# A pre-norm attention and FFN block on one core: 273 softmax denominators summed by VectorE, tokens in two buffers by turns, bias added in place

## The reference, cut to what matters

```
x = x + attn(layernorm(x));  x = x + ffn(layernorm(x))
attn: q, k, v = split(x @ Wqkv)
      num = exp((rotated q) (rotated k)^T / 4)
      den = sum over all keys of exp(q k^T / 4)       # plain q and k, no mask
      y = where(causal, num / den, 0) @ v;  return y @ Wout + bout
ffn:  relu(x @ Ws1)^2 @ Ws2 + routed part (trunc of the top-2 weights)
```

## Time and profile before

| | |
|---|---|
| median of 3 runs | 1646.12 us (1645.99 to 1646.13) |
| the profiled execution | 1646.03 us, its span 1644.4 us |
| ACT busy | 97% |
| PE busy (modelled ends, pipelined) | 91% |
| DVE busy | 51% |
| POOL busy | 32% |
| mean granted TensorE clock | 0.997 |

### The profile page before, as it was taken

How to read it: one execution, slowest core, us unless ns; L and a number is a source line. 1 busy time by engine, 2 the same in 40 slices (tenths; PEclk the granted TensorE clock), 3 DMA queues, 4 the chain that set the end, 5 groups by cost and what they waited for, 6 DMA issues and landing times.

```text
span 1644.4 us, 26290 instructions
## 1 busy us (share of the span) xinstructions
PE 1503.6 (91%) x8594; PEld 614.6 (37%) x8594; DVE 845.8 (51%) x1949; ACT 1591.2 (97%) x2651; POOL 530.2 (32%) x919
## 2 busy tenths in 40 slices
PE   8899999999999989999899999989989999999988
PEld 6334333333333333333333332433333333333325
DVE  5334434665346653566445554565534665346515
ACT  2999999999999999999999999999999999999995
POOL 3334133432234322343333323324223432234310
PEclk9999999999999999999999999999999999999999
DMA  5532233331434313343233333333243331433310
GB/s 164 154 104 87 78 106 116 121 107 50 132 116 132 116 36 126 116 132 106 78 110 119 113 96 105 114 116 97 84 141 110 121 99 62 132 106 116 103 39 27
DMA packets 95392, 172.10 MB, mean 105 GB/s; under 512 B 15696, under 2 KB 82256, under 8 KB 83152
## 3 DMA queue, kind: packets, MB, share of 16 engines
q1 hardware_dynamic: 94656, 169.55, 33.0%
q10 hardware_dynamic: 592, 0.79, 0.2%
HBM read 111.55 MB, written 58.72 MB: 104 GB/s over the span
## 4 chain that ended last, share of the span: by engine, by line
ACT 88%; PE 6%; issue 3%; DVE 1%; POOL 0%; DVEq 0%; DMA 0%; POOLq 0%
ACT scores L546 57%; ACT probs L556 27%; ACT probs L558 3%; PE scores L621 2%; PE y_ps L650 1%; PE side L602 1%; PE side L660 1%; PE scores L628 0%; POOL v_sb L424 0%; DVEq L931 0%; DMA qk_parts<-parts 0%; PE scores L679 0%; PE scores L808 0%; PE scores L669 0%; PE side L679 0%
## 5 line engine op out<-in xcount | busy, mean ns | idle before, releaser
L546 ACT ACTIVATE scores<-scores 128x1024 f32<-128x1024 f32 x1024 | 1068.0, 1124 | 16.1 <-PE scores L621 15.7
L621 PE MATMUL scores<-stack 96*128 96x512 bf16 x2048 | 579.9, 382 | 63.0 <-ACT scores L546 36.3
L556 ACT ACTIVATE probs<-scores 128x1024 f32<-128x1024 f32 x512 | 491.8, 1113 | 1.7 <-PE scores L628 1.7
L628 PE MATMUL scores<-stack 96*128 96x512 bf16 (+3 forms) x1536 | 332.4, 328 | 43.3 <-ACT scores L546 35.0
L443 POOL TENSOR_SCALAR_AFFINE_SELECT probs<-probs 128x256 f32<-128x256 f32 (+1 forms) x640 | 241.2, 404 | 378.5 <-ACT probs L556 218.0
L650 PE MATMUL y_ps<-probs,v_sb 128*32 128x512 f32 (+3 forms) x3072 | 329.0, 500 | 5.1 <-POOL probs L443 5.1
L621 PEld LDWEIGHTS scores<-stack 96*128 96x128 bf16 x2048 | 153.5, 97 | 460.6 <-ACT scores L546 201.3
L546 ACT ACTIVATION_READ_ACCUMULATOR scores<-scores 128x1 f32 x1024 | 302.7, 296 | 0.0
L453 POOL TENSOR_TENSOR parts<-rest,parts 128x512 bf16<-128x512 f32 x124 | 143.2, 1155 | 293.3 <-DVE parts L998 293.3
L628 PEld LDWEIGHTS scores<-stack 96*128 96x128 bf16 x1536 | 117.1, 98 | 290.2 <-ACT scores L546 150.0
L451 POOL TENSOR_TENSOR rot<-raw,cos_sb 128x512 f32<-128x512 f32 x62 | 89.4, 1441 | 388.5 <-DVEq L1008 388.5
(11 more groups left out here) (140 smaller groups left out, 1150.8 us busy)
## 6 DMA issues: line engine op xcount, KB each, us to landing
stack<-qk_parts SPq DMA_DIRECT2D x756, 128.0 KB, 2.6
qk_parts<-parts SPq DMA_DIRECT2D x127, 384.0 KB, 2.6
out<-x_mid SPq DMA_DIRECT2D x32, 256.0 KB, 2.9
x_in<-in_L_attn_x SPq DMA_DIRECT2D x7, 1024.0 KB, 5.3
stack<-qk_parts SPq DMA_DIRECT2D x18, 64.0 KB, 2.3
x_in<-in_L_attn_x SPq DMA_DIRECT2D x2, 512.0 KB, 4.5
probs<-in_L_attn_Wqkv SPq DMA_DIRECT2D x1, 512.0 KB, 5.8
cos_sb<-in_cos SPq DMA_DIRECT2D x1, 512.0 KB, 6.5
```

What stands on the lines that cost most here:

```text
L546: nc.scalar.activation(src, src, ACT.Exp, scale=SCALE, accum_out=den[:, g % 2, i, j:j + 1]).then_inc(exp_done, 1)
L556: nc.scalar.activation(probs[:, chunk % 2, j, :], src, ACT.Exp, scale=SCALE).then_inc(exp_done, 1)
L621: mm = nc.tensor.matmul(tile[:, half * HALF:(half + 1) * HALF], q[:, j, i * P:(i + 1) * P], k[:, j, half * HALF:(half + 1) * HALF], start= ...
L628: mm = nc.tensor.matmul(tile[:, col:col + n], k[:, h, i * P:(i + 1) * P], q[:, h, q0:q0 + n], start=True, stop=True)
```

## The change

1. 273 of the 1024 den steps no longer accumulate. ScalarE writes their exponentials to one of two new SBUF tiles (`sum_tiles`) with a plain activation, and VectorE adds the two halves with one scalar_tensor_tensor that has an accumulator output (`sum_den`), three steps later in its queue (`SUM_LAG`). ScalarE waits, before it writes one such tile, until the one two before was summed. Per unit: 7, 8, 9 and 11 of them in the four groups, 8 in the first and 3 in the last unit.
2. All tables of the order are new.
3. The product with the cosines moves from POOL to VectorE (read from PSUM), the shuffle moves from the `turn` to the `qk` job, and `raw` is gone.
4. Tokens are in two buffers used by turns; attention is added in place; the bias is added in place by POOL in unit 0 of the batch (8 separate instructions at steps 2 to 37). The load of the next tokens no longer waits for POOL's copy; from the second batch on it waits for `tokens_used`.
5. A drain before each reciprocal; `ones` has one column; several tiles share memory.

The core of the diff:

```diff
-ORDER = [5, (0,), 4, (1,), 3, (2,), 7, (3,), 6, (4,), 7]
-ORDER_FIRST = [16, (0,), 1, (1,), 1, (2,), 1, (3,), 1, (4,), 12]
-ORDER_LAST = [0, (0,), 4, (1,), 0, (2,), 7, (3,), 11, (4,), 10]
+ORDER = [5, (0,), 5, (1,), 3, (2,), 7, (3,), 5, (4,), 7]
+ORDER_FIRST = [14, (0,), 0, (1,), 3, (2,), 0, (3,), 9, (4,), 6]
+ORDER_LAST = [1, (0,), 1, (1,), 3, (2,), 2, (3,), 18, (4,), 7]
+SUM_SLOTS, SUM_LAG = 2, 3
+SUMMED = [
+    (6, 7, 10, 12, 16, 17, 27),
+    (1, 4, 15, 21, 22, 24, 25, 27),
+    (5, 9, 11, 16, 18, 19, 21, 26, 28),
+    (3, 6, 9, 11, 12, 15, 21, 22, 25, 27, 28),
+    (2, 5, 17),
+    (1, 7, 12, 17, 19, 23, 24, 26),
+]
...
 SIDE = [
-    {0: ("v", 0), 4: ("qk", 0), 8: ("v", 1), 12: ("v", 2), 14: ("turn", 1), 20: ("qk", 2), 28: ("turn", 3),
-     30: ("v", 3), 35: ("norm", 0), 38: ("norm", 1)},
...
+    {0: ("qk", 0), 4: ("v", 0), 8: ("v", 1), 12: ("v", 2), 18: ("turn", 1), 21: ("qk", 2), 24: ("turn", 3),
+     30: ("v", 3), 38: ("norm", 0), 41: ("norm", 1), 47: ("acc", 0)},
...
+    {1: ("qk", 0), 6: ("ffn", 1), 10: ("route", 2), 11: ("turn", 1), 13: ("qk", 2), 18: ("ffn", 2),
+     24: ("norm", 0), 26: ("turn", 3), 28: ("norm", 1), 31: ("acc", 0), 33: ("acc", 1), 38: ("ffn", 3),
+     40: ("acc", 2), 47: ("xt", 0), 49: ("xt", 1)},
...
-COPY = (1, 43)
+BIAS = (0, (2, 7, 12, 17, 22, 27, 32, 37))
...
+        sum_tiles = sb("sum_tiles", [P, SUM_SLOTS, C])
+        tokens = [sb(f"tokens{i}", [P, NB, D]) for i in range(2)]
...
+                        if not first:
+                            sp.wait_ge(tokens_used, at(b, 1, 0))
+                            sp.sem_inc(held["sp"], 1)
+                        sp.dma_start(tokens[(b + 1) % 2][:, :, :], x_v[b + 1]).then_inc(x_loaded, 16)
...
-                if t % 2 == 0:
-                    pool.wait_ge(raw_ready, at(b, 8, 2 * g + t // 2 + 1))
-                    nc.gpsimd.tensor_tensor(rot[:, :], raw[:, :], cos_sb[:, t // 2 * HALF:(t // 2 + 1) * HALF], ALU.mult)
...
+                        if g == BIAS[0] and s in BIAS[1]:
+                            if s == BIAS[1][0]:
+                                pool.wait_ge(xn_ready, at(b, 4, 4))
+                            block = tokens[b % 2][:, BIAS[1].index(s), :]
+                            nc.gpsimd.tensor_tensor(block, block, bias[:, :], ALU.add).then_inc(biased, 1)
...
+                    if s in SUM_AT[unit_of(b, g)]:
+                        k = sums_ahead(b, g) + SUM_AT[unit_of(b, g)][s]
+                        if k >= SUM_SLOTS:
+                            act.wait_ge(summed, k - SUM_SLOTS + 1)
+                        nc.scalar.activation(sum_tiles[:, k % SUM_SLOTS, :], src, ACT.Exp, scale=SCALE).then_inc(exp_done, 1)
+                        return
...
-                    nc.vector.tensor_copy(raw[:, :], side).then_inc(taken["qk"], 1)
-                    dve.drain().then_inc(raw_ready, 1)
-                    split(0, raw[:, :])
+                    nc.vector.tensor_copy(rest[:, :], side)
+                    nc.vector.tensor_tensor(rot[:, :], side, cos_sb[:, cols], ALU.mult).then_inc(taken["qk"], 1)
+                    settle()
+                    nc.vector.tensor_copy(parts[:, 0, 0, :], rest[:, :])
+                    nc.vector.stream_shuffle(turned[:, :], rest[:, :], PARTNER)
+                    settle()
+                    nc.vector.tensor_tensor(rest[:, :], rest[:, :], parts[:, 0, 0, :], ALU.subtract)
                     middle(0)
                 else:
-                    nc.vector.stream_shuffle(turned[:, :], raw[:, :], PARTNER)
-                    settle()
...
+            def sum_den(b, g, s):
...
+                dve.wait_ge(exp_done, at(b, G * NSTEP, g * NSTEP + s + 1))
+                nc.vector.scalar_tensor_tensor(tile[:, 0:HALF], tile[:, 0:HALF], 0.0, tile[:, HALF:C], ALU.add, ALU.add,
+                                               accum_out=den[:, g % 2, i, j:j + 1]).then_inc(summed, 1)
...
             def reciprocals(b, g):
                 dve.wait_ge(exp_done, at(b, G * NSTEP, (g + 1) * NSTEP))
+                settle()
...
+                        if s - SUM_LAG in SUM_AT[unit_of(b, g)]:
+                            sum_den(b, g, s - SUM_LAG)
```

More of the change, by code:

```diff
@@ L90, in unit_of, with summed_steps, sums_ahead @@
     return G if b == B - 1 and g == G - 1 else G + 1 if b == 0 and g == 0 else g
+SUM_SLOTS, SUM_LAG = 2, 3
+SUMMED = [
[6 rows of a table added]
+]
+def summed_steps(steps, chosen):
+    dens = [s for s, x in enumerate(steps) if x[0] == "den"]
+    return {dens[d]: k for k, d in enumerate(chosen)}
+SUM_AT = [summed_steps(steps, chosen) for steps, chosen in zip(STEPS, SUMMED)]
+def sums_ahead(b, g):
+    return sum(len(SUM_AT[unit_of(n // G, n % G)]) for n in range(b * G + g))
 PIECES = [(0, 0), (0, 1), (1, 0), (1, 1), (2, 0), (2, 1), (2, 2), (3, 1), (3, 0), (3, 2), (4, 0), (4, 1)]
 PV_STEPS = [
[6 rows of a table removed]
[6 rows of a table added]
 ]
@@ L104 @@
 Y_FIRST, Y_LAST = [(0, 0), (3, 0)], [(3, 1), (4, 1)]
-TAKE_Y = [47, 42, 37, 42, 36, 39]
+TAKE_Y = [39, 35, 39, 44, 33, 40]
 LOW_LAG = 3
-RECIPROCALS = (32, 25, 16, 25)
+RECIPROCALS = (30, 35, 9, 24)
 SIDE = [
-    {0: ("v", 0), 4: ("qk", 0), 8: ("v", 1), 12: ("v", 2), 14: ("turn", 1), 20: ("qk", 2), 28: ("turn", 3),
-     30: ("v", 3), 35: ("norm", 0), 38: ("norm", 1)},
[L119 to L128, removed]
-    {0: ("qk", 0), 4: ("v", 0), 8: ("turn", 1), 10: ("v", 1), 14: ("qk", 2), 18: ("v", 2), 22: ("turn", 3), 24: ("v", 3)},
@@ L130 @@
+    {1: ("acc", 3), 4: ("xt", 2), 5: ("xt", 3), 8: ("qk", 0), 15: ("ffn", 4), 18: ("ffn", 5), 21: ("turn", 1),
+     23: ("qk", 2), 28: ("turn", 3), 34: ("ffn", 6), 37: ("ffn", 7)},
+    {1: ("acc", 3), 5: ("ffn", 4), 7: ("ffn", 5), 10: ("ffn", 6), 19: ("ffn", 7), 36: ("end", 0),
+     39: ("end", 1), 40: ("end", 2), 47: ("end", 3), 48: ("end", 4)},
+    {2: ("qk", 0), 8: ("v", 0), 11: ("turn", 1), 12: ("v", 1), 18: ("qk", 2), 22: ("v", 2), 26: ("turn", 3),
+     29: ("v", 3)},
 ]
@@ L257, in block @@
         chunk_used = sem("chunk_used")
+        summed = sem("summed")
         y_ready = sem("y_ready")
@@ L482, in batch @@
                     for s in range(NSTEP):
-                        if (g, s) == COPY:
-                            if not first:
-                                pool.wait_ge(x_acc_used, at(b, 1, 0))
-                            else:
-                                pool.wait_ge(x_first, 16)
-                                pool.wait_ge(x_loaded, 16)
-                            for i in range(NB):
-                                last_copy = nc.gpsimd.tensor_tensor(x_acc[:, i, :], x_in[:, i, :], bias[:, :], ALU.add)
-                            last_copy.then_inc(x_copied, 1)
+                        if g == BIAS[0] and s in BIAS[1]:
[3 more added lines that the diff above has]
+                            nc.gpsimd.tensor_tensor(block, block, bias[:, :], ALU.add).then_inc(biased, 1)
                         for c in DIAGONALS:
@@ L816, in end_tile @@
                     pe.wait_ge(weight_ready, at(b, 1, 1))
[L817 removed]
+                    mm = nc.tensor.matmul(side[0:1, 0:NB], ones[:, :], weight[:, :], start=True, stop=True)
                 mm.then_inc(end_full, 1)
@@ L1074, in acc_tile @@
                 src = side.rearrange("p (i d) -> p i d", i=2)
-                into = x_mid if pair else x_acc
-                nc.vector.tensor_tensor(into[:, blocks, :], src, x_acc[:, blocks, :], ALU.add).then_inc(taken["acc"], 1)
+                into = x_mid if pair else tokens[b % 2]
+                nc.vector.tensor_tensor(into[:, blocks, :], src, tokens[b % 2][:, blocks, :], ALU.add).then_inc(taken["acc"], 1)
                 if pair:
                     if t == 3:
-                        dve.drain().then_inc(x_acc_used, 1)
+                        dve.drain().then_inc(tokens_used, 1)
                     else:
@@ L1150, in end_tile @@
                     blocks = slice(2 * t, 2 * t + 2)
-                    nc.vector.tensor_tensor(x_mid[:, blocks, :], side.rearrange("p (i d) -> p i d", i=2), x_acc[:, blocks, :],
+                    nc.vector.tensor_tensor(x_mid[:, blocks, :], side.rearrange("p (i d) -> p i d", i=2), tokens[b % 2][:, blocks, :],
                                             ALU.add).then_inc(end_taken, 1)
```

60 lines of the change are left out of this document (30 added, 30 removed), and 12 rows, old and new, of the table PV_STEPS.

## The result

The change takes 1631.42 us (median of 5 runs, 1628.03 to 1635.59) against 1646.12 us before: ratio 0.991, 95% interval 0.990 to 0.993. It is faster by 14.7 us where 33 were forecast, and the time lies outside the stated range of 1608 to 1624 us. The profiled execution is one of 1631.42 us, span 1629.8.

A forecast was written before the change was run, and what follows sets the result against it. ScalarE's own pace was taken to bound the kernel (ACT busy for 97% of the span). From 1646.0 us, minus 34.7 for the accumulator read-outs, plus 1.5 for late sums, came 1612.8 us; range 1608 to 1624 us.

The forecast's parts named there:

- 273 denominators without accumulator: On ScalarE's path: each plain activation saves the 0.127 us accumulator read-out, 34.7 us in all.
- The sums on VectorE: Each sum costs VectorE 0.86 us (0.70 to 1.73), 235 us for all 273.
- The cosine product moves: From POOL to VectorE: 43 us more on VectorE, 89 less on POOL; with shorter neighbours, VectorE nets 16 us less.
- VectorE in all: VectorE's total load: 1065 us (1020 to 1302) of some 1613, 66%, leaving room on average.
- Where a late sum would be felt: ScalarE waiting for a free sum tile at 23 close-spaced places: 1.5 us charged, bounds 0 and 12 us.
- Tokens and bias: Token loads and in-place bias on SP's and POOL's queues: no effect on the time.
- TensorE, no lack: In unit 0, the heaviest, TensorE needs 43 us of the 48.3 that ScalarE needs, so it holds nothing up.
- The first unit: First numerator after 14 denominators, waiting some 2 us for DMA; the 1.0 us its 8 sums count was left in.
- A: VectorE's answer comes late, behind POOL's masks or long jobs; ScalarE or TensorE waits: 1618 to 1630 us, chance 0.15.
- the likeliest case: The forecast itself, ScalarE's saving nearly whole: 1608 to 1618 us, chance 0.75.

The follow-up runs named there:

- run 1: The change, with each of the 273 sums on VectorE adding one column instead of 512 (denominators then wrong): 1620.99 us.
- run 2: The change, with one product with v (chunk 3, piece 1) of unit 0 at step 40 in place of 38: 1623.89 us.
- run 3: The change, with POOL's 8 bias additions early, at steps 2 to 19 of unit 0: 1622.79 us.
- run 7: The change, with each sum done by a VectorE reduction over 1024 columns instead of adding two halves: 1634.04 us.
- run 5: The change without any sum, all 1024 denominators accumulated by ScalarE: 1657.25 us, ratio 1.0051 to the kernel before.
- run 13: The change without any sum and with the first acc job back at step 3 of unit 1: 1647.62 us, ratio 1.0013 to before.
- run 17: The change, with unit 0's product with v at step 40, the bias early and a few small filler matmuls on TensorE: 1617.35 us, ratio 0.9813 to before.
- run 11: The kernel before, with only the first acc job moved from step 3 of unit 1 to step 47 of unit 0: 1646.55 us, ratio 1.0001.
- run 14: The change, with three small unused matmuls at each of ten steps where TensorE had least to do: 1630.15 us.
- run 9: The change, with unit 0's product with v at step 40, the bias early and acc at step 4 of unit 1: 1620.73 us.

## Why the prediction was wrong

- *273 denominators without accumulator, 34.7 us*: right. Measured 273 x 0.126 = 34.4, and the idle time before these activations is 0.1 us.
- *The sums on VectorE, 0.86 us* (its three terms add up to 0.85): right, 0.77 + 0.08. Alone a sum takes 0.68, by the rows of batch 3, and a plain addition 0.70. The Trainium skill, in Vector Engine (DVE) Microarchitecture Reference, section Points that are easy to get wrong, gives half throughput for two SBUF sources that are not bf16. These rows do not show it: halved, a sum would take some 1.2 us (an estimate from that page).
- *The cosine product moves*: right on VectorE (0.68; the subtraction 0.69). POOL lost 55 us of busy time, not 89, as its other instructions became longer: the third parts by 26 us, the bias by 9.
- *VectorE in all*: 1018 us, below the 1065 and 2 us under the lower bound of 1020. The lengths of its rows grew by some 218 us, near the 219 that I had; its busy time, which counts overlapping rows once, grew by 172. I had added lengths to a busy time.
- *Where a late sum would be felt, 1.5 us*: **this step failed.** I looked for the price only where ScalarE waits for `summed`, and there it is indeed nothing. I had measured the exclusion and used it only to make the sum dearer. It works the other way too: a sum holds POOL, and POOL carries the masks, behind which TensorE and then ScalarE stand. 10.2 us, shown by runs 1, 2, 3 and 7.
- *Tokens and bias, nothing*: failed with it. I said what it removes from SP's queue and not what it puts in POOL's: two bias additions in front of the masks of chunk 3. I also did not put the new step 38 of the product beside step 35 of its last numerator, though both stood in the diff.
- *TensorE, no lack*: right for its amount of work, and blind to its clock. The kernel before had 0.997, and I took it for given; the new order has stretches after which it falls. By run 5 against 13 the change without sums lost some 9 us to it. In the change itself it is 4 to 5, an estimate from 1.1 us per 0.001 and a mean clock over its runs of 0.992 against 0.996 to 0.997.
- *The first unit*: the first numerator started at 51.18 where I had 51.2. But the unit's shortage grew by 2.1 us, 3.1 of its 6.4 in front of the first numerator (I had some 2); its sums gave 1.0 and it took 1.1 us longer.
- The rivals: A had the right witnesses (POOL's masks behind the sums) and the wrong place, ScalarE's wait for a slot; its 1618 to 1630 is near the result. I gave it 0.15 and cut the range in its middle. What the forecast wanted exists: with both misplacements mended and the clock kept up (run 17) the time is 1617.4 us, inside the likeliest case.

Open: what, besides the stretch that the moved acc job thins, decides in which batches the clock falls there (run 11 has the same thin stretch and one dip), and the 5 us of waits of 0.1 to 0.4 us spread over the units.

## What to carry to other kernels

When work moves to an engine that can shut another out, price it on both: list what is queued on the other engine behind each instruction that can be held up, and who waits for that. When an order is rewritten, look at what is *thinned* as well as at what is crowded: TensorE's clock fell after light stretches, though not after all of them, and a few useless matmuls in them kept it up. Whether those pay is less clear: beside tight steps they cost what they saved (run 14), and away from them the gain over a kernel without them was within the scatter (runs 9 and 17). And if ScalarE accumulates, take the price of it from distances between starts (0.126 us), not from the row of the read-out (0.2 to 0.37 us).

## What the runs showed of the hardware

- A VectorE instruction with two SBUF inputs and a POOL instruction that reads SBUF shut each other out, in both directions: a sum of 0.68 us took 1.64 behind POOL, a third part of 1.16 us took 1.61 behind a sum. With one SBUF input (the reduction, 1.21 us for 1024 columns) or with one column, POOL's rows were undisturbed (1.157 us). The Trainium skill's page SBUF — State Buffer (section SBUF: two separate sides) describes it as a lock on a shared pair of ports; these rows agree.
- A scalar_tensor_tensor of 128x512 with accumulator takes 0.68 us and its read-out 0.08, most of it beside the next instruction.
- TensorE's granted clock fell from 1.00 to 0.50 for 3.4 us at a time (in some runs 6.8) and cost the kernel about 1 us for each 3.4. In the change it fell once behind a wait of 3.51 us; at the other places the engine had only been less busy, as with 2.23 of 3.40 us ahead of the fall at 290.4, while ScalarE was busy throughout. Stretches as thin in other batches brought no fall (2.00 of 3.40 us at 483.5). With the fillers (3.11 of 3.4 us at the start of unit 1) there was none in units 1 and 2.
